# Inverse norms of queries and keys on GpSimd instead of ScalarE, and a new weaving of the instruction streams

## The chip, the cores and the metric

The kernel runs on one core of a Trainium2 chip. A core has five engines that run their own instruction lists in order: TensorE (PE, matrix multiplies and transposes), VectorE (DVE), ScalarE (ACT, one function per element), GpSimd (POOL) and SyncE (SP, which only issues DMA transfers here). They meet through semaphores. The metric is the device time of one execution in microseconds (us). Before the change it was 2464.19 us, the median of 3 runs (2455.86 to 2464.42).

## The reference, cut to what matters

The input is 16 elements (`b` below) of 512 tokens by 128 features. Each goes through a selective state space layer (the Mamba kind), then through two local attention layers with a feed-forward part each:

```python
x = x + layernorm(mamba(layernorm(x)))
h = layernorm(x)
for l in range(2):                          # "front" is l = 0, "back" is l = 1
    h = layer(h, ...)
x = x + layernorm(h)

# inside a layer
q, k, v = split(shift_token(h) @ wqkv)      # 8 heads of 64
q = q / clip(norm(q), 1e-12) * q_scale      # the part that the change moves
k = k / clip(norm(k), 1e-12) * k_scale
q, k = rotary_xpos(q, k)
o = local_attention(q * 8, k, v)            # windows of 64 tokens
h = h + o @ wo
h = h + feed_forward(shift_token(h))        # layernorm, gated GELU
```

The factor 8 on the queries is folded into the inverse norm. The state space layer is a scan over 512 steps for 256 channels with 16 states each.

## The kernel before, in words

The work on one element is cut into streams, each with a letter. `E` (enter) normalises the input, projects it and runs the short convolution; it ends with the step sizes. `F` (steps) makes the step sizes and their products with the input on POOL and sends them to memory. `M` (state) is the scan: 32 pieces of 128 partitions by 512 steps. For each piece POOL multiplies `dbu<-spread,bc` (the "feed"), ACT makes `da` by an exponential, DVE runs the scan `hs`, POOL multiplies `gy<-hs,bc` (the "read out"), and PE adds four of those into `y_sum`. `M` ends with two gates on POOL, a projection, two layer norms and `xs`, which is the input of `A` (front, layer 0). After it comes `B` (back, layer 1) and `C` (end: last norm, residual, store). `S` stores what `E` made for `M`.

While element `b` is in `B`, `b+1` is in `A`, `b+2` in `M` and `b+3` in `E`. Every engine works through one word per element. A word such as `A1 B2 M1` says: one step of stream A, two of B, one of M. So the order on each engine is written out by hand in the table `ORDER`, and an instruction that waits holds everything behind it on its engine. `AHEAD` says how many elements a stream is ahead, and `weave` plays the word; what is left of a stream at the end of a word is issued there. The streams in the code are functions named after engine and stream, for instance `act_attention` or `pool_state`.

A and B share no buffers. E shares PSUM bank and SBUF buffers with B: `x_pad` lies in B's `q_t`, `dt` and `du` in B's `k_t`, `dt_abs` in B's `m2`.

The inverse norms of a pair of token tiles (16 values per partition, 4 pairs in each of A and B) go through three engines. DVE sums squares (`ss`, line 879). POOL clips the sum from below (`clip`, line 952). ACT takes the logarithm (`lg`, line 810) and the exponential with scale -0.5 (`rn`, lines 815 and 817, the latter with a bias of log 8 for queries). POOL then multiplies the rotated tile by it (`normalise`, `kr<-kr,rn`, line 960). PE transposes the result, and ACT copies it to `q_t` or `k_t` (line 831). The sums of squares come from `square` on ACT (line 796) and the rotation from three DVE instructions per tile (lines 892, 896, 906). The projections are on line 703.

Of the kernel before, what the change touches and what calls it, by code (L numbers as in the profile page):

```python
# [15 lines left out]
P = 128  # L16
# [25 lines left out]
AHEAD = {"C": -1, "B": 0, "A": 1, "M": 2, "F": 2, "E": 3, "S": 3}  # L42
ORDER = {
# [4 lines left out]
    "act": (  # L48
# [4 lines left out]
    "dve": (  # L53
# [4 lines left out]
    "pool": (  # L58
        "F4 C1 A2 B1 A1 M2 B1 M2 B2 M3 B1 M1 A1 M1 B1 M1 B1 M1 A1 B1 M2 A1 M2 A1 B1 M1 B1 A1 B2 M3 A1 M3 A1 M1 A2 "
        "M44"),  # L60
    "sp": (
        "M1 F2 M5 A1 M1 B1 M1 E1 B1 M3 A1 M6 C1 M5 S3 B1"),
# [30 lines left out]
def weave(word, **streams):  # L93

    for part in word.split():
        for _ in range(int(part[1:]) if part[0] in streams else 0):
            next(streams[part[0]], None)
    for s in streams.values():
        for _ in s:
            pass  # L100


def build(nc, a, out):
    with ExitStack() as ctx:
# [35 lines left out]
        eps, log8 = (columns[:, n:n + 1] for n in range(2))  # L140
# [14 lines left out]
        class Attention:  # L155


            def __init__(self, n, banks, pr):
# [8 lines left out]
                self.lg = sb(f"lg{n}", [P, 8, HEADS])  # L167
# [416 lines left out]
        def act_state(E, e, b):  # L584
            if b > 0:
                E.wait_ge(*y_normed(b - 1))
            else:
                E.wait_ge(*a_made(0))
# [15 lines left out]
        def dve_state(E, e, b):  # L604
# [7 lines left out]

            for s in range(NSCAN):
# [164 lines left out]
        def act_attention(E, e, b, w, l):  # L778
# [10 lines left out]
            def square(take):  # L789
                n = ROPE.index(take)  # L790
                if entry and n == 0:
                    E.wait_ge(*e_turned(b + 2))
                E.wait_ge(*w.projected(b, projections.index(take)))
                if n > 1:
                    E.wait_ge(*w.summed(b, n // 2 - 1))
                e.activation(w.sq[:, n % 2, :], bank_of(take)[:, :], ACT.Square).then_inc(w.squared.sem, 1)  # L796
# [7 lines left out]

            def inverse_norms(g):

                part = lambda x: x[:, 2 * g:2 * g + 2, :]
                E.wait_ge(*w.clipped(b, g))
                E.use_table(EXP_LN)
# [3 lines left out]
                E.use_table(EXP_LN)  # L813
                if g % 2:
                    op = e.activation(part(w.rn), part(w.lg), ACT.Exp, scale=-0.5)
                else:
# [17 lines left out]
            for take in "q0 q1 v0 n0 k0 v1 k1 Q0 n1 Q1 q2 q3 v2 K0 n2 k2 K1 v3 k3 Q2 n3 Q3 K2 K3".split():  # L834
# [6 lines left out]
                elif take[0] == "n":  # L841
                    yield from inverse_norms(int(take[1]))
# [105 lines left out]
        def pool_attention(E, e, b, w):  # L948
            def clip(g):

                E.wait_ge(*w.summed(b, g))
                e.tensor_scalar(w.ss[:, 2 * g:2 * g + 2, :], w.ss[:, 2 * g:2 * g + 2, :], TINY, None, ALU.max).then_inc(
                    w.clipped.sem, 1)
# [9 lines left out]
            for take in "c0 q0 q1 c1 k0 k1 c2 q2 q3 c3 k2 k3".split():  # L963
                if take[0] == "c":
                    clip(int(take[1]))
# [169 lines left out]
        def dve_constants(E, e):  # L1135
            for column, value in ((eps, EPS), (log8, math.log(8.0))):
# [24 lines left out]
        def program(name, streams, once=None, at=0):  # L1161


            def body(e):
                E = Engine(e)
                for k in range(-3, B + 1):
                    if k == at and once:
                        once(E, e)
                    weave(ORDER[name], **{letter: stream(E, e, k + AHEAD[letter])
                                          for letter, stream in streams.items() if 0 <= k + AHEAD[letter] < B})  # L1170
# [9 lines left out]
        with nc.Block() as block:  # L1180
            block.sync(program("sp", dict(C=sp_end, B=sp_back, A=sp_front, M=sp_state, F=sp_steps, E=sp_enter, S=sp_spill)))
# [102 lines left out]
```

## Time and profile before

| what | value |
|---|---|
| median of 3 runs | 2464.19 us |
| the profiled execution's own time | 2461.61 us |
| its span, first to last instruction | 2459.8 us |
| PE busy | 1893.9 us (77%) |
| DVE busy | 1892.7 us (77%) |
| ACT busy | 1778.1 us (72%) |
| POOL busy | 1711.4 us (70%) |
| mean granted TensorE clock | 0.943 of full speed |

The busy shares are averages over the whole span. No engine is near 100%, so the page alone does not name a bound; within one element the engines take turns at being nearly full. Steady state repeats about every 140 us: the same pieces stand at 999.85 and at 1139.59 us. The chain of waits, followed back from the end, is 38% PE, 23% DVE, 13% ACT and 8% POOL.

### The profile page before, as it was taken

Reading aid. Unit: us, or ns where it says so; the run is one execution under the profiler, and the core shown is the slowest. Engines: PE = TensorE matmul, PEld = TensorE weight load, DVE = VectorE, ACT = ScalarE, POOL = GpSimd, SP = SyncE. Lnnn points to the kernel's source line nnn. Section 1 sums busy time; section 2 is a strip of 40 time slices with the busy share of each in tenths; the row PEclk is TensorE's granted clock in tenths of the full one; section 3 lists DMA queues with packets and bytes.
Section 4 is the critical chain, followed back from the end, with each engine's and each line's share of the span. In section 5 each row is a group of like instructions: output and inputs, shape, how many; then the busy total and the mean of one; then the engine's idle time right before and its main releaser. Section 6 shows DMA issues by size and latency. Waiting matters only on the chain.

```text
span 2459.8 us, 44075 instructions
## 1 busy us (share of the span) xinstructions
PE 1893.9 (77%) x15808; PEld 1114.3 (45%) x15936; DVE 1892.7 (77%) x3477; ACT 1778.1 (72%) x3955; POOL 1711.4 (70%) x1540
## 2 busy tenths in 40 slices
PE   2156778797878879797878879697888879787865
PEld 0013345353635445363635445363645545363634
DVE  3557797978879797988878797988879797887442
ACT  2245778696978878696878878696877869685644
POOL 1969595977959596886959596885959597792010
PEclk9977999899999989999999999999999989999988
DMA  4444443535344343534544353534543353531000
GB/s 162 126 120 115 112 105 104 132 83 146 103 130 117 100 121 92 134 86 131 129 129 103 103 124 96 138 87 130 130 115 99 110 127 90 137 99 33 17 20 9
DMA packets 126346, 261.09 MB, mean 106 GB/s; under 512 B 26928, under 2 KB 59696, under 8 KB 125872
## 3 DMA queue, kind: packets, MB, share of 16 engines
q1 hardware_dynamic: 126128, 258.27, 39.6%
q8 instruction: 126, 2.06, 0.4%
q14 instruction: 92, 0.75, 0.1%
HBM read 185.42 MB, written 42.99 MB: 93 GB/s over the span
## 4 chain that ended last, share of the span: by engine, by line
PE 38%; DVE 23%; ACT 13%; issue 9%; POOL 8%; DMA 4%; SPq 0%; DVEq 0%; POOLq 0%; ACTq 0%
DVE hs L618 6%; DVE m L892 4%; PE f_bank L342 4%; PE b_bank L342 4%; DVE kr L906 3%; POOL gy L663 3%; DMA spread<-steps 3%; POOL dbu L646 3%; ACT da L594 3%; PE b_bank L703 3%; PE f_bank L746 3%; PE y_sum L571 2%; DVE b_bank L896 2%; PE b_bank L773 2%; DVE ss L879 2%
## 5 line engine op out<-in xcount | busy, mean ns | idle before, releaser
L618 DVE TENSOR_TENSOR_SCAN hs<-da,dbu 128x512 f32<-128x512 f32 x512 | 622.2, 1215 | 127.1 <-POOL dbu L646 82.0
L663 POOL TENSOR_TENSOR gy<-hs,bc 128x512 f32<-128x512 f32 x512 | 652.1, 1274 | 41.5 <-DVE hs L618 31.2
L646 POOL TENSOR_TENSOR dbu<-spread,bc 128x512 f32<-128x512 f32 x512 | 651.5, 1274 | 9.1 <-DMA spread<-steps 9.0
L594 ACT ACTIVATE da<-spread,rest 128x512 f32<-128x512 f32 x512 | 359.4, 702 | 159.0 <-DVE hs L618 135.1
L703 PE MATMUL b_bank<-rest,h_t 128*128 128x512 f32 x384 | 227.9, 694 | 96.6 <-DVE kr L906 92.5
L960 POOL TENSOR_TENSOR kr<-kr,rn 128x512 f32<-128x512 f32 x256 | 264.8, 1043 | 42.3 <-ACT rn L817 37.0
L703 PE MATMUL f_bank<-rest,h_t 128*128 128x512 f32 x384 | 217.6, 665 | 72.1 <-DVE kr L906 64.2
L571 PE MATMUL y_sum<-gy,rest 128*32 128x512 f32 x1024 | 147.0, 649 | 92.4 <-POOL gy L663 92.3
L342 PE MATMUL f_bank<-first,kr 128*128 128x128 f32 x768 | 128.4, 298 | 78.9 <-DVE kr L906 49.8
L342 PE MATMUL b_bank<-first,kr 128*128 128x128 f32 x768 | 123.7, 296 | 57.8 <-DVE kr L906 41.8
L1106 POOL TENSOR_TENSOR xs<-xs,v 128x512 f32<-128x512 f32 x16 | 18.9, 1183 | 213.3 <-ACT xs L337 213.3
L417 POOL TENSOR_TENSOR k_t<-k_t,m 128x512 f32<-128x512 f32 x32 | 40.0, 1270 | 178.6 <-ACT m L494 178.6
L342 PEld LDWEIGHTS f_bank<-first,kr 128*128 128x128 f32 x768 | 93.3, 151 | 146.4 <-DVE kr L906 70.4
L857 ACT ACTIVATE late<-b_bank,mx 128x128 f32<-128x128 f32 x512 | 140.6, 383 | 23.8 <-DVE mx L922 23.8
L879 DVE TENSOR_REDUCE ss<-sq 128x16 f32<-128x1024 f32 x128 | 154.1, 1204 | 0.0
L342 PEld LDWEIGHTS b_bank<-first,kr 128*128 128x128 f32 x768 | 90.6, 150 | 140.0 <-DVE kr L906 67.3
L703 PEld LDWEIGHTS b_bank<-rest,h_t 128*128 128x128 f32 x384 | 70.7, 214 | 171.5 <-DVE kr L906 127.8
L857 ACT ACTIVATE sq<-f_bank,mx 128x128 f32<-128x128 f32 x512 | 144.0, 393 | 4.4 <-DVE mx L922 4.4
L703 PEld LDWEIGHTS f_bank<-rest,h_t 128*128 128x128 f32 x384 | 73.2, 212 | 158.4 <-DVE kr L906 92.4
L90 ACT ACT_TABLE_LOAD x82 | 105.2, 1283 | 20.4 <-DVE mv_enter L315 7.3
L892 DVE TENSOR_TENSOR m<-f_bank,tab 128x512 f32<-128x512 f32 x128 | 87.2, 682 | 39.1 <-ACT sq L796 39.0
L892 DVE TENSOR_TENSOR m<-b_bank,tab 128x512 f32<-128x512 f32 x128 | 87.2, 681 | 30.6 <-ACT sq L796 30.6
(168 smaller groups left out, 4748.2 us busy)
## 6 DMA issues: line engine op xcount, KB each, us to landing
spread<-steps SPq DMA_DIRECT2D x256, 512.0 KB, 5.1
vs<-v SPq DMA_DIRECT2D x96, 260.0 KB, 5.9
bc<-bc_rows SPq DMA_DIRECT2D x32, 512.0 KB, 6.2
steps<-k_t SPq DMA_DIRECT2D x32, 512.0 KB, 2.7
gate<-gates SPq DMA_DIRECT2D x32, 512.0 KB, 5.7
gates<-kr SPq DMA_DIRECT2D x16, 512.0 KB, 3.4
gates<-late SPq DMA_DIRECT2D x16, 512.0 KB, 4.3
vs<-v SPq DMA_DIRECT2D x32, 130.0 KB, 4.5
```

Of the source, the lines that this page charges most:

```text
L90: self.e.preload_act_table_set(name)
L342: op = e.transpose(bank[:, n * P:(n + 1) * P], src(n), ident[:, :])
L571: op = e.matmul(y_sum[32 * j:32 * j + 32, :], sel[:, w, :], gy[:, 2 * j + k, :], start=w == 0 and k == 0, stop=w == 1 and k == 1, skip_gro ...
L594: e.activation(da[:, :], spread[:, slot(b, s // 2), 0, :], ACT.Exp, scale=a_neg[:, s:s + 1]).then_inc(decayed.sem, 1)
L618: e.tensor_tensor_scan(hs[:, s % 2, :], da[:, :], dbu[:, s % 2, :], 0.0, ALU.mult, ALU.add).then_inc(scanned.sem, 1)
L646: e.tensor_tensor(dbu[:, s % 2, :], spread[:, slot(b, s // 2), 1, :], bc[:, s % 2, :], ALU.mult).then_inc(fed.sem, 1)
L663: e.tensor_tensor(gy[:, s % 8, :], hs[:, s % 2, :], bc[:, 2 + s % 2, :], ALU.mult).then_inc(read_out.sem, 1)
L703: e.matmul(bank[:, :], w.h_t[:, t * P:(t + 1) * P], wqkv[:, l, part * INNER:(part + 1) * INNER], start=True, stop=True).then_inc(w.project ...
L857: op = e.activation(w.pr[:, hd % 2, p, :], X[hd % 2][:, p * P:(p + 1) * P], ACT.Exp, bias=w.mx[:, hd, p:p + 1])
L879: e.tensor_reduce(w.ss[:, 2 * g:2 * g + 2, :], w.sq[:, :, :].rearrange("p n (h d) -> p n h d", h=HEADS), AX, ALU.add).then_inc(w.summed.se ...
L892: e.tensor_tensor(halves(w.m2[:, n % 2, :]), halves(bank[:, :])[:, :, ::-1, :], table[1], ALU.mult).then_inc(w.rotated.sem, 1)
L960: e.tensor_tensor(x, x, w.rn[:, n, :].unsqueeze(2).to_broadcast([P, HEADS, DH]), ALU.mult).then_inc(w.normed.sem, 1)
```

## The change

It does three things.

1. The logarithm and exponential of the inverse norms leave ACT (`inverse_norms` is gone, and 8 steps of each ACT attention stream with it). POOL now follows its clip with a `tensor_tensor` of the operation power: `ss` to the power of a column that holds -1/2. To keep the factor 8 of the queries, ACT squares them with a scale of 0.125. Buffer `lg` is gone.
2. `weave` no longer starts and ends each stream within a word. A stream is now one chain over all 16 elements, the word is repeated until all chains are out, and a second string says how many turns a stream lets pass at the start. `AHEAD` is gone. The set-up work of ACT and DVE (`act_tables`, `dve_tables`) moves to the first step of `M`.
3. All five words are new. They begin at another point of the element's cycle, and most of their text is the old order rotated to it.

```diff
 class Engine / weave
-def weave(word, **streams):
-    for part in word.split():
-        for _ in range(int(part[1:]) if part[0] in streams else 0):
-            next(streams[part[0]], None)
-    for s in streams.values():
-        for _ in s:
-            pass
+def weave(word, late, **chains):
+    late = {part[0]: int(part[1:]) for part in late.split()}
+    while chains:
+        for part in word.split():
+            for _ in range(int(part[1:])):
+                if late[part[0]]:
+                    late[part[0]] -= 1
+                elif part[0] in chains and next(chains[part[0]], chains) is chains:
+                    del chains[part[0]]
...
-        eps, log8 = (columns[:, n:n + 1] for n in range(2))
+        eps, root = (columns[:, n:n + 1] for n in range(2))
...
-                e.activation(w.sq[:, n % 2, :], bank_of(take)[:, :], ACT.Square).then_inc(w.squared.sem, 1)
+                e.activation(w.sq[:, n % 2, :], bank_of(take)[:, :], ACT.Square, scale=0.125 if take[0] == "q" else 1.0).then_inc(
+                    w.squared.sem, 1)
...
-            def inverse_norms(g):
-                part = lambda x: x[:, 2 * g:2 * g + 2, :]
-                E.wait_ge(*w.clipped(b, g))
-                e.activation(part(w.lg), part(w.ss), ACT.Ln).then_inc(w.logged.sem, 1)
-                yield
-                E.wait_ge(*w.logged(b, g))
...
-                    op = e.activation(part(w.rn), part(w.lg), ACT.Exp, scale=-0.5, bias=log8)
-                op.then_inc(w.inverse.sem, 1)
-                yield
...
-            for take in "q0 q1 v0 n0 k0 v1 k1 Q0 n1 Q1 q2 q3 v2 K0 n2 k2 K1 v3 k3 Q2 n3 Q3 K2 K3".split():
+            for take in "q0 q1 v0 k0 v1 k1 Q0 Q1 q2 q3 v2 K0 k2 K1 v3 k3 Q2 Q3 K2 K3".split():
...
         def pool_attention(E, e, b, w):
-            def clip(g):
+            def inverse_roots(g):
+                part = lambda x: x[:, 2 * g:2 * g + 2, :]
                 E.wait_ge(*w.summed(b, g))
-                e.tensor_scalar(w.ss[:, 2 * g:2 * g + 2, :], w.ss[:, 2 * g:2 * g + 2, :], TINY, None, ALU.max).then_inc(
-                    w.clipped.sem, 1)
+                e.tensor_scalar(part(w.ss), part(w.ss), TINY if g % 2 else TINY / 64, None, ALU.max).then_inc(w.clipped.sem, 1)
+                E.wait_ge(*w.clipped(b, g))
+                e.tensor_tensor(part(w.rn), part(w.ss), root.unsqueeze(2).to_broadcast([P, 2, HEADS]), ALU.pow).then_inc(
+                    w.inverse.sem, 1)
...
         "sp" word
-        "M1 F2 M5 A1 M1 B1 M1 E1 B1 M3 A1 M6 C1 M5 S3 B1"),
+        "M1 B1 M3 E1 M1 B1 M2 A1 M1 A1 M9 S3 M1 B1 F1 M1 F1 M2 C1 M1",
+        "A4 B9 C3 E0 F0 M18 S0"),
```

How the order moved is seen best in the instruction lists. On POOL, at the start of a new pair of attentions (steady state), this stood in a row before: `xs<-xs,v` ends stream C, `ss<-ss` is a clip, `kr<-kr,rn` a normalisation.

```order
L1106 TENSOR_TENSOR xs<-xs,v 128x512
L952 TENSOR_SCALAR ss<-ss 128x16
L960 TENSOR_TENSOR kr<-kr,rn 128x512
L952 TENSOR_SCALAR ss<-ss 128x16
L960 TENSOR_TENSOR kr<-kr,rn 128x512
L646 TENSOR_TENSOR dbu<-spread,bc 128x512 x2
L960 TENSOR_TENSOR kr<-kr,rn 128x512
L663 TENSOR_TENSOR gy<-hs,bc 128x512
```

And this stands there now; `rn<-ss,columns` is the power.

```order
L1098 TENSOR_TENSOR xs<-xs,v 128x512
L942 TENSOR_SCALAR ss<-ss 128x16
L944 TENSOR_TENSOR rn<-ss,columns 128x16
L952 TENSOR_TENSOR kr<-kr,rn 128x512 x2
L653 TENSOR_TENSOR dbu<-spread,bc 128x512
L942 TENSOR_SCALAR ss<-ss 128x16
L944 TENSOR_TENSOR rn<-ss,columns 128x16
L653 TENSOR_TENSOR dbu<-spread,bc 128x512
L952 TENSOR_TENSOR kr<-kr,rn 128x512
L670 TENSOR_TENSOR gy<-hs,bc 128x512
```

Eight powers per element are new on POOL, each directly behind its clip; both normalisations of A's first pair now come before the first feed.

On ACT, from the norm of `x1` (end of stream M) to the first squares of the next pair of attentions, this stood before. `m<-m` are the four functions of stream F, `h_t` is the shifted input of an attention (`f_bank` is A, `b_bank` is B), `lv_out` and `rs_out` belong to C.

```order
L326 ACTIVATE rs_x<-lv_x 128x4
L337 ACTIVATE xs<-x,mr_x,rs_x 128x128 x4
L484 ACTIVATE m<-b_bank,first 128x512
L491 ACTIVATE m<-m 128x512 x2
L494 ACTIVATE m<-m 128x512 x2
L783 ACTIVATE h_t<-f_bank 64x512
L785 ACTIVATE h_t<-f_bank 64x511
L783 ACTIVATE h_t<-b_bank 64x512
L785 ACTIVATE h_t<-b_bank 64x511
L796 ACTIVATE sq<-f_bank 128x512
L322 ACTIVATE lv_out<-mv_out,columns 128x4
L326 ACTIVATE rs_out<-lv_out 128x4
```

This stands there now.

```order
L330 ACTIVATE rs_x<-lv_x 128x4
L488 ACTIVATE m<-b_bank,first 128x512
L495 ACTIVATE m<-m 128x512 x2
L498 ACTIVATE m<-m 128x512 x2
L341 ACTIVATE xs<-x,mr_x,rs_x 128x128 x4
L326 ACTIVATE lv_out<-mv_out,columns 128x4
L330 ACTIVATE rs_out<-lv_out 128x4
L790 ACTIVATE h_t<-f_bank 64x512
L792 ACTIVATE h_t<-f_bank 64x511
L790 ACTIVATE h_t<-b_bank 64x512
L792 ACTIVATE h_t<-b_bank 64x511
L803 ACTIVATE sq<-f_bank 128x512
```

The norm of `x1` moved behind F, and C's two small instructions moved ahead of the attention inputs. DVE has the matching move: `stat_out` and `mv_out` now stand before the last addition of A's feed-forward, not behind it.

On SP the load of the read-out factors (`bc<-bc_rows`, the second of its kind) stood right behind the first two groups of step sizes:

```order
L376 DMA steps<-k_t 128x2x512
L379 DMA steps<-k_t 128x2x512
L514 DMA spread<-steps 128x1x1024 x2
L508 DMA bc<-bc_rows 128x1x1024
L514 DMA spread<-steps 128x1x1024 x2
```

Now the store of the finished element, which waits for `xs<-xs,v` on POOL, stands between them:

```order
L383 DMA steps<-k_t 128x2x512
L518 DMA spread<-steps 128x1x1024 x2
L1115 DMA out_dram<-xs 128x4x128
L512 DMA bc<-bc_rows 128x1x1024
L518 DMA spread<-steps 128x1x1024
```

The second load of factors and all behind it now wait for the end of C.

## Rows read from the trace of the kernel before

**Rows 1.** Busy time by stage of one element (front, heads, tail), in us.

```profile
1121.00:1182.00 61.00, 43.07 (x239) 21.22 (x240) 56.34 (x89) 40.49 (x93) 50.61 (x52) 0.92 0.56 139
1182.00:1235.00 53.00, 48.19 (x641) 34.48 (x645) 46.44 (x91) 48.30 (x120) 50.82 (x42) 1.00 0.38 101
1235.00:1261.00 26.00, 24.60 (x117) 13.29 (x114) 14.53 (x40) 21.89 (x38) 6.07 (x5) 1.00 0.28 83
```

**Rows 2.** The residual addition that ends M: durations, first and last start.

```profile
L674 POOL TENSOR_TENSOR x<-gy,x x16: 1261/1270/1274, 152.0 to 2221.8; 128x512 f32<-128x512 f32 x16
```

**Rows 3.** The chain of waits from 1129 to 1181 us: start, length, what.

```profile
1129.20 0.59 DVE m L892
...
1156.17 0.60 ACT k_t L831
1156.77 0.11 ACT lg L810
...
1156.91 0.32 ACT rn L817
...
1157.29 1.04 POOL kr L960
...
1179.99 1.01 POOL kr L960
```

**Rows 4.** Groups by line and shape: count, busy us, mean ns, idle before.

```profile
L663 POOL TENSOR_TENSOR gy<-hs,bc 128x512 f32<-128x512 f32 x512 | 652.1, 1274 | 41.5 <-DVE hs L618 31.2 <-DMA bc<-bc_rows 5.0 <-PE y_sum L571 1.0
L960 POOL TENSOR_TENSOR kr<-kr,rn 128x512 f32<-128x512 f32 x256 | 264.8, 1043 | 42.3 <-ACT rn L817 37.0 <-ACT rn L815 3.1 <-DVE kr L906 0.6
L952 POOL TENSOR_SCALAR ss<-ss 128x16 f32<-128x16 f32 x128 | 31.4, 245 | 93.2 <-DVE ss L879 92.6
L810 ACT ACTIVATE lg<-ss 128x16 f32<-128x16 f32 x128 | 27.3, 213 | 49.2 <-POOL ss L952 48.5
L817 ACT ACTIVATE rn<-lg,columns 128x16 f32<-128x16 f32 x64 | 19.7, 307 | 2.1
L815 ACT ACTIVATE rn<-lg 128x16 f32<-128x16 f32 x64 | 13.8, 216 | 2.0
```

**Rows 5.** POOL in order of time, front stage: start, length, idle before.

```profile
1131.00 0.24 POOL L952 TENSOR_SCALAR ss<-ss 128x16 f32<-128x16 f32 x1 [1.09 <-DVE ss L879]
1131.92 1.04 POOL L960 TENSOR_TENSOR kr<-kr,rn 128x512 f32<-128x512 f32 x1 [0.67 <-ACT rn L817]
...
1142.67 0.24 POOL L952 TENSOR_SCALAR ss<-ss 128x16 f32<-128x16 f32 x1 [1.39 <-DVE ss L879]
...
1153.04 0.24 POOL L952 TENSOR_SCALAR ss<-ss 128x16 f32<-128x16 f32 x1 [0.54 <-DVE ss L879]
...
1157.29 1.04 POOL L960 TENSOR_TENSOR kr<-kr,rn 128x512 f32<-128x512 f32 x1 [1.77 <-ACT rn L817]
...
1178.52 0.24 POOL L952 TENSOR_SCALAR ss<-ss 128x16 f32<-128x16 f32 x1 [0.16 <-DVE ss L879]
```

**Rows 6.** Who waited for whom from 1121 to 1182 us: total, times, longest.

```profile
DVE m L892 <- ACT sq L796: 3.5, 3, 1.7
```

**Rows 7.** End of M and start of the next attentions, in order of time.

```profile
1115.35 1.65 ACT L337 ACTIVATE xs<-x,mr_x,rs_x 128x128 f32<-128x128 f32 x4 [0.64 <-DVE mr_x L331]
...
1117.48 1.14 ACT L491 ACTIVATE m<-m 128x512 f32<-128x512 f32 x2
...
1120.48 0.60 PE L342 MATMUL f_bank<-first,xs 128*128 128x128 f32 x4
```

**Rows 8.** The second load of factors, C's last step, and the first read out.

```profile
1128.22 0.60 SPq L508 DMA_DIRECT2D bc<-bc_rows  x1
...
1128.73 1.18 POOL L1106 TENSOR_TENSOR xs<-xs,v 128x512 f32<-128x512 f32 x1 [4.58 <-ACT xs L337]
...
1137.78 1.27 POOL L663 TENSOR_TENSOR gy<-hs,bc 128x512 f32<-128x512 f32 x1
```

**Rows 9.** DMA issues on the page: count, KB each, us from issue to landing.

```profile
bc<-bc_rows SPq DMA_DIRECT2D x32, 512.0 KB, 6.2
```

More of the change, by code:

```diff
@@ L35 @@
 ROPE = "q0 q1 k0 k1 q2 q3 k2 k3".split()
-AHEAD = {"C": -1, "B": 0, "A": 1, "M": 2, "F": 2, "E": 3, "S": 3}
 ORDER = {
     "pe": (
[3 rows of a table removed]
[4 rows of a table added]
     "act": (
[4 rows of a table removed]
-    "dve": (
[4 rows of a table removed]
[5 rows of a table added]
+    "dve": (
[5 rows of a table added]
     "pool": (
-        "F4 C1 A2 B1 A1 M2 B1 M2 B2 M3 B1 M1 A1 M1 B1 M1 B1 M1 A1 B1 M2 A1 M2 A1 B1 M1 B1 A1 B2 M3 A1 M3 A1 M1 A2 "
-        "M44"),
+        "M2 F4 C1 A3 M1 B1 M1 B1 M2 B1 M1 B2 M3 A1 M2 A1 M2 B2 M1 A1 M1 B2 M1 A1 M1 A1 B3 M2 A1 M5 A3 M42",
+        "A12 B24 C3 F0 M2"),
     "sp": (
-        "M1 F2 M5 A1 M1 B1 M1 E1 B1 M3 A1 M6 C1 M5 S3 B1"),
+        "M1 B1 M3 E1 M1 B1 M2 A1 M1 A1 M9 S3 M1 B1 F1 M1 F1 M2 C1 M1",
+        "A4 B9 C3 E0 F0 M18 S0"),
 }
@@ L166, in __init__ @@
                 self.ss = sb(f"ss{n}", [P, 8, HEADS])
-                self.lg = sb(f"lg{n}", [P, 8, HEADS])
                 self.rn = sb(f"rn{n}", [P, 8, HEADS])
@@ L587, in act_state @@
             else:
+                act_tables(E, e)
                 E.wait_ge(*a_made(0))
@@ L611, in skip @@
                                        ALU.add).then_inc(skipped.sem, 1)
+            if b == 0:
+                dve_tables(E, e)
             for s in range(NSCAN):
@@ L803, in value @@
                 e.activation(w.v[:, t, :, 0:DH], heads(bank_of(take)[:, :]), ACT.Copy).then_inc(w.v_copied.sem, 1)
-            def inverse_norms(g):
-                part = lambda x: x[:, 2 * g:2 * g + 2, :]
-                E.wait_ge(*w.clipped(b, g))
-                E.use_table(EXP_LN)
-                e.activation(part(w.lg), part(w.ss), ACT.Ln).then_inc(w.logged.sem, 1)
-                yield
-                E.wait_ge(*w.logged(b, g))
[L813 to L816, printed above, removed]
-                    op = e.activation(part(w.rn), part(w.lg), ACT.Exp, scale=-0.5, bias=log8)
-                op.then_inc(w.inverse.sem, 1)
-                yield
             def channel_major(take):
@@ L840, in act_attention @@
                     yield
-                elif take[0] == "n":
-                    yield from inverse_norms(int(take[1]))
                 else:
@@ L964, in pool_attention @@
                 if take[0] == "c":
-                    clip(int(take[1]))
+                    inverse_roots(int(take[1]))
                 else:
@@ L1135, in dve_constants @@
         def dve_constants(E, e):
-            for column, value in ((eps, EPS), (log8, math.log(8.0))):
+            for column, value in ((eps, EPS), (root, -0.5)):
                 e.memset(column, value)
@@ L1159, in act_tables, with program, elements @@
             e.activation(a_neg[:, :], a_neg[:, :], ACT.Exp).then_inc(a_exp.sem, 1)
-        def program(name, streams, once=None, at=0):
+        def program(name, **streams):
+            def elements(E, e, stream):
+                for b in range(B):
+                    yield from stream(E, e, b)
             def body(e):
                 E = Engine(e)
[L1166 to L1170, printed above, removed]
+                weave(*ORDER[name], **{letter: elements(E, e, stream) for letter, stream in streams.items()})
                 if name == "sp":
@@ L1180, in build @@
         with nc.Block() as block:
-            block.sync(program("sp", dict(C=sp_end, B=sp_back, A=sp_front, M=sp_state, F=sp_steps, E=sp_enter, S=sp_spill)))
-            block.gpsimd(program("pool", dict(C=pool_end, B=pool_back, A=pool_front, M=pool_state, F=pool_steps)))
-            block.scalar(program("act", dict(C=act_end, B=act_back, A=act_front, M=act_state, F=act_steps, E=act_enter),
-                                 act_tables, -2))
-            block.vector(program("dve", dict(C=dve_end, B=dve_back, A=dve_front, M=dve_state, E=dve_enter), dve_tables, -2))
-            block.tensor(program("pe", dict(B=pe_back, A=pe_front, M=pe_state, E=pe_enter)))
+            block.sync(program("sp", C=sp_end, B=sp_back, A=sp_front, M=sp_state, F=sp_steps, E=sp_enter, S=sp_spill))
+            block.gpsimd(program("pool", C=pool_end, B=pool_back, A=pool_front, M=pool_state, F=pool_steps))
+            block.scalar(program("act", C=act_end, B=act_back, A=act_front, M=act_state, F=act_steps, E=act_enter))
+            block.vector(program("dve", C=dve_end, B=dve_back, A=dve_front, M=dve_state, E=dve_enter))
+            block.tensor(program("pe", B=pe_back, A=pe_front, M=pe_state, E=pe_enter))
 FIRST = [("ident", (P,)), ("w_in", (2 * DI,)), ("conv_w", (NH2, NCONV)), ("conv_b", (NH2,)), ("w_x", (NH2, 2 * NS + RANK)),
```

25 rows, old and new, of the table ORDER are left out of this document.

## The prediction

> **What bounds the kernel now.** I read the busy times by stage first, then the chain of waits, then POOL in order of time.
>
> One element takes about 140 us and falls into three stages [rows 1]; the columns are PE, weight loads, DVE, ACT, POOL. In the front stage (projections, rotation, norms) DVE is busy 56.3 of 61 us and POOL 50.6. In the stage of the heads POOL is busy 50.8 of 53, ACT 48.3 and PE 48.2. In the tail PE is busy 24.6 of 26 and POOL 6.1. So the edit falls in the front stage, where DVE is fullest, and it loads POOL, the fullest engine of the next one.
>
> POOL's idle time in the front stage is at its beginning: it cannot start before the first clip at 1131.00, and from there it runs almost without a break to 1181.0, 50.0 us [rows 3, 5]. The chain of waits goes through the other engines up to 1156, then ACT's copy of a key tile, logarithm and exponential, and from 1157.29 to 1181.0 it is POOL alone, 23.7 us [rows 3]. Five gaps interrupt the 50.0 us: 0.67 + 1.39 + 0.54 + 1.77 + 0.16 = 4.53 us [rows 5]. Two of them (0.67 and 1.77) end with ACT's exponential. The 1.77 is the telling one: the clip of that pair was over at 1153.28, but ACT's logarithm stood behind a copy that ran only at 1156.17, so the inverse norm was there at 1157.2 [rows 3, 5].
>
> **Taken from ACT.** Per full element 8 logarithms and 8 exponentials: over the run 27.3 + 19.7 + 13.8 = 60.8 us of busy time [rows 4], 3.8 us per element, and 48.5 / 16 = 3.0 us in which ACT stood for the clip [rows 4]. Little of this is on the path: where the chain crosses them it is 0.11 + 0.32 us [rows 3]. It frees ACT's queue, so squares come earlier, and DVE's wait for squares (3.5 us per front stage [rows 6]) can shrink. I count nothing for it beside POOL's gain below, since both end the same stage; the cap on any gain in the front stage is DVE's idle time there, 61 - 56.3 = 4.7 us [rows 1].
>
> **Added to POOL.** 8 powers of 128x16 per element. No row shows a power. From below: a clip of the same shape takes 245 ns [rows 4]. From above I take a whole 128x512 multiplication, 1274 ns [rows 4]. The nearest row is the clip, same engine and shape; a power is more work on each of the 16 elements. The multiplication by the inverse norm costs 1043 ns for 512 elements [rows 4], 2.0 ns each; with five times that for a power, 16 x 10 = 160 ns, I take 0.40 us as an estimate. Eight make 3.2 us, all of it inside POOL's 50 us run.
>
> The Trainium skill, "GPSIMD Engine Reference", Performance versus the Vector engine, puts a two-input elementwise body at about 2.6 cycles per element and data-dependent branching at about 12, and says to keep elementwise work off this engine. At its 1.2 GHz the first is 2.2 ns; the row gives 2.0, so they agree. By 12 cycles a power of 16 elements would be 0.16 us over the fixed part; by the plain body the whole would be about 0.28 us, and the eight 2.2 us.
>
> **The stall that goes.** With the power behind its clip on POOL, the two gaps that end with ACT cannot occur. The other three end with DVE's sum of squares; as POOL gets busier in between, they close too. Sum over the run: -4.53 + 3.2 = -1.3 us per element. What is late next: DVE, full in this stage, and POOL itself. If the powers cost more than 4.53 / 8 = 0.57 us, POOL's run gets longer than before.
>
> **What the new words do.** On DVE the sum of squares of A's first pair has one instruction fewer ahead of it, a step of 0.6 us (a 128x512 instruction of the rotation holds the chain for 0.59 [rows 3]). POOL's run begins that much earlier: -0.6 us. C's small instructions go ahead of the attention inputs on ACT, and C's statistics ahead of A's last addition on DVE, so POOL's `xs` comes earlier, and ACT waits less for it before it copies B's values. That wait is off the chain; I count it at zero.
>
> The norm of `x1` moves behind F on ACT. It began at 1115.35; one function of about 0.6 us and F, two pairs of 1.1 us each, now stand ahead, so it would end near 1119.8, and PE reads it at 1120.48 [rows 7]. The work of PE that lies before that transpose hides it with 0.7 us to spare; before there were 3.5. F, no longer behind 1.65 us of norm [rows 7], starts some 1.5 us earlier, and so do the stores of the step sizes.
>
> SP's second load of factors was issued at 1128.22. It now waits for C's last POOL step, over at 1129.91, so about 2 us later. Such a load takes 6.2 us [rows 9]: it lands near 1136.5, and the first read out was at 1137.78 [rows 8]. Hidden by 1.3 us; if `xs` is late, M's start pays it one for one. Behind this load stand two groups of step sizes, of which the first pieces are already there.
>
> **Start and end.** M ends 16 times, from 152.0 to 2221.8 us [rows 2]. Full front stages with A, B and M together number 14. After 2222 there is one A with a B, then a B alone; there POOL is not full, and a pair costs the hop from clip to normalisation. That was 0.92 us (1131.00 to 1131.92 [rows 5]); now it is 0.24 + 0.40 plus a small gap, about 0.7. Twelve hops save 2 us. The repeated word changes neither which stream runs beside which nor how many instructions there are, so I count the new weaving itself at zero, with 5 us either way.
>
> **The sum.** (-1.3 - 0.6) x 14 = -27, and -2 at the end: 2461.6 - 29 = 2433 us. The profiled execution's own 2461.6 is 0.1% below the median of the runs shown, 2464.2, so the figure holds for both.
>
> **Rivals.**
>
> *The power is expensive (slower).* One mechanism: a power of 1.0 us, between the bounds. Place: POOL's run in the front stage. Price: 8.0 - 4.53 - 0.6 = +2.9 us per element, x 14 = +40, so 2502 us; at 1.27 us it would be +5.1 x 14 = +71, so 2533. It decides from 0.57 us (0.65 with the earlier start). For it: the chain is POOL alone for the last 23.7 us, three clips lie in that part, and POOL has only 2.2 us of room in the stage of the heads. Against it: M's end has 3.5 us of room before PE, so POOL may drag scan work into the tail before the cycle lengthens; this may swallow part.
>
> *No change.* The powers take just what the gaps give, or DVE's 56.3 us in the front and PE's 24.6 in the tail hold the cycle wherever POOL stands: 2461 us, within 0.5% of now. For it: neither engine loses an instruction. Against it: the chain does not go through DVE after 1157.
>
> *The words bring more.* ACT and DVE, no longer held by POOL's clips, give most of the 4.7 us cap: -3.3 us per element, x 14 = -46, so 2415 us. For it: ACT loses 6.8 us of work and waiting in this stage. Against it: the 3.5 us that DVE waited for squares partly end with PE's projections, which the edit does not touch.
>
> *The change doesn't do what it says.* Excluded: the instruction lists show 8 powers and no logarithm or exponential for them, and as many loads of function tables as before.
>
> **How the numbers follow.** Chances: my forecast 0.38, the words bring more 0.12, no change 0.17, expensive power 0.33. A difference of 0.5% (12 us) is about what a measurement can tell from none. So faster 0.50, same 0.17, slower 0.33. The range must reach into the expensive power: up to 2506, a power of 1.0 us with a few us; what lies above is the dearer part of that case. Below it reaches to 2402, the third rival with words and start 13 us better. The forecast's own range is 2415 to 2448.
>
> **What would show it.** The power's mean on its own row decides most: 0.40 right, over 0.65 wrong. POOL from its first clip of a front stage to its last normalisation: 50.0 us before, about 48.7 after. The wait of the normalisation for ACT (40.1 us) must be gone, and so ACT's 48.5 us for the clip. ACT's busy time falls by 61 us; POOL's rises by 128 x 0.40 = 51. DVE's wait for POOL's feeds must not rise; if it does, POOL became the bound. PE's transpose of `xs` must still not wait for the norm of `x1`, nor the first read out for the second load of factors. M's ends must span less than the 2069.8 us that lie between the first and the last now. I am wrong if that distance grows.

## The result, and the profile of the changed kernel

The changed kernel takes 2773.14 us (median of 4 runs, 2771.90 to 2775.28), against 2464.31 us before (median of 4, 2455.86 to 2468.20): 1.126 times as long, 95% interval 1.1243 to 1.1276. The profiled execution's span is 2770.1 us, +310 on before's 2459.8. I had forecast 2433 us and a range up to 2506. The place that I gave in the first rival was right, POOL's run in the front stage; the price of a power was not, and that price alone carries the result.

The groups by line, on the page of the changed kernel (busy us, mean ns of one, idle before and what ended it), which answer to [rows 4]:

```profile
L625 DVE TENSOR_TENSOR_SCAN hs<-da,dbu 128x512 f32<-128x512 f32 x512 | 623.6, 1218 | 299.7 <-POOL dbu L653 245.7
L944 POOL TENSOR_TENSOR rn<-ss,columns 128x16 f32<-128x16 f32 x128 | 374.2, 2924 | 10.7
L346 PE MATMUL b_bank<-first,kr 128*128 128x128 f32 x768 | 149.5, 341 | 292.2 <-POOL kr L952 272.4
L952 POOL TENSOR_TENSOR kr<-kr,rn 128x512 f32<-128x512 f32 x256 | 263.9, 1042 | 5.4
```

A power of 128x16 takes 2.924 us, more than two 128x512 multiplications (1.27 us). The 128 of them are 374.2 us of POOL. The normalisation waits for nobody now: 5.4 us of idle time before it, 42.3 before [rows 4]. Instead DVE's scan waits 245.7 us for POOL's feeds and PE's transposes of stream B wait 272.4 us for POOL's normalised tiles. Before, these two waits were 82.0 and 10.0 us:

```profile
L618 DVE TENSOR_TENSOR_SCAN hs<-da,dbu 128x512 f32<-128x512 f32 x512 | 622.2, 1215 | 127.1 <-POOL dbu L646 82.0 <-ACT da L594 36.8 <-POOL gy L663 3.6
L342 PE MATMUL b_bank<-first,kr 128*128 128x128 f32 x768 | 123.7, 296 | 57.8 <-DVE kr L906 41.8 <-POOL kr L960 10.0 <-ACT v L803 4.9
```

The chain that ended last, by engine and by line: before, POOL had 8% of it, now 43%, and the power alone has 13%. The 43% is not all the power's doing: in the run below with a multiplication in its place POOL has 34% of the chain, and that kernel is not slower than before. What the power adds is its own 13%.

```profile
POOL 43%; PE 27%; DVE 11%; ACT 6%; issue 6%; DMA 0%; POOLq 0%; SPq 0%; DVEq 0%; ACTq 0%
POOL rn L944 13%; POOL gy L670 12%; POOL dbu L653 11%; POOL kr L952 6%; DVE hs L625 4%; PE f_bank L346 3%; PE b_bank L346 3%; PE y_sum L575 2%; DVE m L882 2%; PE f_bank L986 2%; PE b_bank L992 2%; PE f_bank L983 2%; PE f_bank L992 1%; PE b_bank L736 1%; ACT late L847 1%
```

The stages of one element, cut at the same events as in [rows 1] (columns PE, weight loads, DVE, ACT, POOL, then the granted clock of PE): the front took 61 us and takes 81, the other two 54 and 26 as against 53 and 26. In the front POOL is busy 72.2 us where it was 50.6; DVE, which I had named as the fullest there, has 58.0 us of work in it (56.3 before) and 20 us more for it.

```profile
1256.00:1337.00 81.00, 46.36 (x238) 23.61 (x239) 57.97 (x82) 37.68 (x78) 72.20 (x58) 0.85 0.42 109
1337.00:1391.00 54.00, 49.08 (x638) 36.54 (x644) 44.34 (x90) 47.29 (x116) 51.55 (x42) 0.97 0.39 102
1391.00:1417.00 26.00, 25.08 (x121) 13.38 (x120) 16.02 (x47) 22.61 (x40) 7.22 (x6) 1.00 0.20 63
```

POOL in order of time in that front stage (start, length), which answers to [rows 5]: eight powers, each just behind its clip, the last before the two normalisations with which the stage ends.

```profile
1266.13 0.25 POOL L942 TENSOR_SCALAR ss<-ss 128x16 f32<-128x16 f32 x1 [1.35 <-DVE ss L869]
1266.46 2.92 POOL L944 TENSOR_TENSOR rn<-ss,columns 128x16 f32<-128x16 f32 x1
1269.47 2.04 POOL L952 TENSOR_TENSOR kr<-kr,rn 128x512 f32<-128x512 f32 x2
1271.47 1.26 POOL L653 TENSOR_TENSOR dbu<-spread,bc 128x512 f32<-128x512 f32 x1
1272.81 0.25 POOL L942 TENSOR_SCALAR ss<-ss 128x16 f32<-128x16 f32 x1
1273.15 2.92 POOL L944 TENSOR_TENSOR rn<-ss,columns 128x16 f32<-128x16 f32 x1
...
1332.81 2.92 POOL L944 TENSOR_TENSOR rn<-ss,columns 128x16 f32<-128x16 f32 x1
1335.81 2.04 POOL L952 TENSOR_TENSOR kr<-kr,rn 128x512 f32<-128x512 f32 x2
```

From the first clip at 1266.13 to the end of the first of the last two normalisations (1336.86) it is 70.7 us; before, the same stretch was 50.0. The account closes: 8 powers of 2.92 and 8 small gaps of 0.08 before them are 24.0, less the five gaps of [rows 5], 4.53, plus one new idle time of 0.76 us, make +20.3 of the measured +20.7. The ends of M, against [rows 2]:

```profile
L681 POOL TENSOR_TENSOR x<-gy,x x16: 1262/1272/1277, 150.5 to 2525.5; 128x512 f32<-128x512 f32 x16
```

First to last it is 2375.0 us, 2069.8 before: +305.2 over 15 elements, 20.3 each. That this distance grows was my sign of being wrong. With +6.6 behind the last M and -1.5 before the first, that is the whole +310.

### The profile page after: what moved, and what is told of

Same layout as the page of the kernel before. It is cut to its first block, busy times and chain, and to the rows that moved or that the text cites. A ratio compares the mean times of both kernels' runs of the same rounds, so it can differ in the third digit from the quotient of the medians.

```text
span 2770.1 us, 43947 instructions
## 1 busy us (share of the span) xinstructions
PE 1967.0 (71%) x15808; PEld 1176.3 (42%) x15936; DVE 1911.2 (69%) x3477; ACT 1728.2 (62%) x3699; POOL 2085.5 (75%) x1668
## 4 chain that ended last, share of the span: by engine, by line
POOL 43%; PE 27%; DVE 11%; ACT 6%; issue 6%; DMA 0%; POOLq 0%; SPq 0%; DVEq 0%; ACTq 0%
POOL rn L944 13%; POOL gy L670 12%; POOL dbu L653 11%; POOL kr L952 6%; DVE hs L625 4%; PE f_bank L346 3%; PE b_bank L346 3%; PE y_sum L575 2%; DVE m L882 2%; PE f_bank L986 2%; PE b_bank L992 2%; PE f_bank L983 2%; PE f_bank L992 1%; PE b_bank L736 1%; ACT late L847 1%
## 5 line engine op out<-in xcount | busy, mean ns | idle before, releaser
L625 DVE TENSOR_TENSOR_SCAN hs<-da,dbu 128x512 f32<-128x512 f32 x512 | 623.6, 1218 | 299.7 <-POOL dbu L653 245.7
L944 POOL TENSOR_TENSOR rn<-ss,columns 128x16 f32<-128x16 f32 x128 | 374.2, 2924 | 10.7
L346 PE MATMUL b_bank<-first,kr 128*128 128x128 f32 x768 | 149.5, 341 | 292.2 <-POOL kr L952 272.4
L346 PE MATMUL f_bank<-first,kr 128*128 128x128 f32 x768 | 156.8, 345 | 173.5 <-DVE kr L896 107.6
L346 PEld LDWEIGHTS b_bank<-first,kr 128*128 128x128 f32 x768 | 105.9, 172 | 389.1 <-issue 329.4
L346 PEld LDWEIGHTS f_bank<-first,kr 128*128 128x128 f32 x768 | 117.0, 179 | 220.9 <-DVE kr L896 125.9
L1098 POOL TENSOR_TENSOR xs<-xs,v 128x512 f32<-128x512 f32 x16 | 18.9, 1181 | 223.2 <-ACT xs L341 223.2
L823 ACT ACTIVATE k_t<-b_bank 128x512 f32<-128x512 f32 x64 | 38.2, 597 | 165.0 <-PE b_bank L346 165.0
```

The lines of the kernel that those rows point to most:

```text
L346: op = e.transpose(bank[:, n * P:(n + 1) * P], src(n), ident[:, :])
L625: e.tensor_tensor_scan(hs[:, s % 2, :], da[:, :], dbu[:, s % 2, :], 0.0, ALU.mult, ALU.add).then_inc(scanned.sem, 1)
L944: e.tensor_tensor(part(w.rn), part(w.ss), root.unsqueeze(2).to_broadcast([P, 2, HEADS]), ALU.pow).then_inc(w.inverse.sem, 1)
```

## The experiments

Three questions: is it the power (its price, or its place), the new words, or the new weaving? The ratios are against the kernel before, with 95% intervals.

### A multiplication in the power's place

```diff
-  e.tensor_tensor(part(w.rn), part(w.ss), root..., ALU.pow)
+  e.tensor_tensor(part(w.rn), part(w.ss), root..., ALU.mult)
```

> The changed kernel with a multiplication in the place of the power (the norms are left out, all instructions and waits stay). Price theory: the instruction takes about 0.25 us, and the time is that of my prediction's formula, 8 x 0.34 - 4.53 - 0.6 = -2.4 us per element x 14: 2420 to 2450 us. Place rival (two dependent GpSimd instructions and the hop to them cost, whatever they compute): above 2550 us.

This kernel leaves the inverse norms out: a multiplication stands where they were made. 2445.82 us, ratio 0.9938 (0.9915 to 0.9960). All else is the changed kernel: same words, waits and number of instructions. The row of that instruction and the scan's wait for feeds:

```profile
L944 POOL TENSOR_TENSOR rn<-ss,columns 128x16 f32<-128x16 f32 x128 | 27.8, 217 | 10.7
L625 DVE TENSOR_TENSOR_SCAN hs<-da,dbu 128x512 f32<-128x512 f32 x512 | 623.0, 1217 | 123.5 <-POOL dbu L653 79.4 <-ACT da L599 37.5 <-issue 5.3
```

The operation alone is worth 2773.1 - 2445.8 = 327.3 us, 2.56 us for each of 128, of the 2.71 by which the two instructions differ. The instruction in its place, with the words and the weaving, is harmless, even 0.6% faster than before.

This run also shows what the new words do to POOL's run in the front stage. From the first clip (1122.97) to the end of the first of the last two normalisations it takes 49.3 us, 50.0 before. All five gaps of [rows 5] are gone; one new idle time stands before the first read out, with no releaser that the profile shows. The ends of M lie 2052.1 us apart, 1.2 us less per element than before:

```profile
1130.67 1.27 POOL L670 TENSOR_TENSOR gy<-hs,bc 128x512 f32<-128x512 f32 x1 [0.94 <-issue]
L681 POOL TENSOR_TENSOR x<-gy,x x16: 1263/1272/1277, 150.6 to 2202.7; 128x512 f32<-128x512 f32 x16
```

### The power with the old words

The kernel before, with the logarithm and exponential gone from ACT (empty steps stand for them, so the words stay as they are) and the power behind the clip on POOL; the factor 8 moves to the squares, as in the change.

```diff
-  e.activation(part(w.lg), part(w.ss), ACT.Ln) ... e.activation(part(w.rn), part(w.lg), ACT.Exp, scale=-0.5)
+  yield; yield                                  # ACT: two empty steps
+  e.tensor_tensor(part(w.rn), part(w.ss), root..., ALU.pow)   # POOL, behind the clip
```

> The kernel before with its own weaving and words; only the edit of the norms is made: power on GpSimd behind the clip, two empty ScalarE steps where logarithm and exponential stood. Price theory: 8 x (2.92 + 0.09) - 4.5 = 19.6 us more per element, x 15 to 16, so 2755 to 2780 us. Order rival: the power alone explains less, so below 2700 us.

2821.24 us, ratio 1.1460 (1.1439 to 1.1480). So the power is at least as dear with the old words, and the new ones take 48 us off it. The time lies 41 us above the range of the price theory (2755 to 2780), so the sum with the measured power was too low here. Per element it is 3.1 us more than in the changed kernel. The trace shows 2.3 of them: the first clip comes 0.6 us later behind the end of M, and POOL's run lasts 72.4 us against 70.7, with two gaps left that DVE's sum of squares ends (0.88 and 1.33 us). The rest is open. The wait that shows it is DVE's for feeds, 336.5 us here against 245.7 in the changed kernel:

```profile
L618 DVE TENSOR_TENSOR_SCAN hs<-da,dbu 128x512 f32<-128x512 f32 x512 | 622.9, 1217 | 403.2 <-POOL dbu L646 336.5
```

### The multiplication with the old words

The same with `ALU.mult` for `ALU.pow`; again the inverse norms are left out.

> The kernel before with its own weaving and words and a multiplication where the power would be (the norms are left out), ScalarE without logarithm and exponential. With e2 it gives the price of the power under the old words; with e3 what the new words are worth when the instruction is cheap. If the hop over ScalarE was what the old words paid for: below before, 2420 to 2450 us. If the old words fit only with the hop: 2455 to 2500 us. In both cases e2 minus e11 should be that of the changed kernel minus e3, about 327 us.

2459.67 us, ratio 0.9987 (0.9978 to 0.9997). With the run above it tests my term "the stall that goes". POOL's rows, and three clips of one front stage:

```profile
L954 POOL TENSOR_TENSOR kr<-kr,rn 128x512 f32<-128x512 f32 x256 | 264.0, 1043 | 2.3
L944 POOL TENSOR_SCALAR ss<-ss 128x16 f32<-128x16 f32 x128 | 31.3, 244 | 96.1 <-DVE ss L870 91.6
L946 POOL TENSOR_TENSOR rn<-ss,columns 128x16 f32<-128x16 f32 x128 | 27.7, 216 | 10.7
...
1140.90 0.24 POOL L944 TENSOR_SCALAR ss<-ss 128x16 f32<-128x16 f32 x1 [1.38 <-DVE ss L870]
...
1152.11 0.24 POOL L944 TENSOR_SCALAR ss<-ss 128x16 f32<-128x16 f32 x1 [0.80 <-DVE ss L870]
...
1176.72 0.24 POOL L944 TENSOR_SCALAR ss<-ss 128x16 f32<-128x16 f32 x1 [0.16 <-DVE ss L870]
```

The idle time before the normalisation falls from 42.3 [rows 4] to 2.3 us, but 27.7 + 10.7 us of new instruction and gap take almost all of it, and the idle time before the clips, which DVE ends, does not close: 96.1 against 93.2. In the front stage the two gaps that ACT ended are gone, the three that DVE ended stand (2.34 us, 2.09 before), and POOL's run is 50.3 us, 50.0 before. I had let all five gaps go; with the old words only two do.

### The new words with ACT's functions

The changed kernel, with logarithm and exponential on ACT again, issued just ahead of the next step of the attention stream, and no power.

```diff
+  E.wait_ge(*w.clipped(b, g)); e.activation(part(w.lg), part(w.ss), ACT.Ln)
+  E.wait_ge(*w.logged(b, g));  e.activation(part(w.rn), part(w.lg), ACT.Exp, scale=-0.5)
-  e.tensor_tensor(part(w.rn), part(w.ss), root..., ALU.pow)
```

> The changed kernel with its weaving and its words, but the logarithm and the exponential back on ScalarE (issued ahead of the step that follows) and no power on GpSimd. Price theory (the 2.92 us of a power on GpSimd's full queue is the whole loss): back to the level of before, 2430 to 2470 us. Order rival (the new words cost a good part of the 309 us): above 2520 us.

2557.57 us, ratio 1.0388 (1.0369 to 1.0407). My price theory failed, and the time lies in the range of the rival (above 2520): I had thought the words independent of where the inverse norm is made. POOL now stands for ACT (42.3 us before [rows 4]):

```profile
L961 POOL TENSOR_TENSOR kr<-kr,rn 128x512 f32<-128x512 f32 x256 | 264.5, 1045 | 120.9 <-ACT rn L820 120.8
```

In the new word of POOL four of the eight clips of a front stage have their own normalisation right behind them. With POOL's own instruction between them POOL waits for nobody, with a hop to ACT and back it stands and holds the scan's feeds meanwhile: DVE waits 113.3 us for them, 79.4 with the multiplication. In one front stage these waits for ACT are 7.6 us, in five places; before they were the 2.4 us of two gaps [rows 5]. The four corners and their partners, in us:

| | logarithm and exponential on ACT | multiplication on POOL | power on POOL |
|---|---|---|---|
| old words | 2461 (before, in the run beside) | 2460 | 2821 |
| new words | 2558 | 2446 | 2773 |

Power less multiplication is 361.6 us in one row and 327.3 in the other. The power is dear with either words; that the two differences should be the same, as I had expected, is off by 34 us.

### The new words with ACT's functions and no clip

The logarithm adds a small constant instead (`bias=tiny`) and waits for DVE's sum alone.

> The new words and the new weaving, logarithm and exponential on ACT ahead of the next step of the stream, and no clip: the logarithm adds a small constant instead, so that it waits for DVE's sum of squares alone and POOL has nothing in that chain before the normalisation. It asks what makes the new words dear with ACT's functions (2557.6 us against 2461). Theory 1, the hop: POOL's clip, placed in the new words just ahead of the normalisations, starts the chain late, and POOL then stands for ACT. Without the clip most of the 96 us are back: 2465 to 2490 us, and POOL's wait of kr for ACT's rn, 120.8 us there, falls below 40. Theory 2, ACT's queue: the functions have no steps of their own in ACT's new word and stand behind copies and exponentials, so that rn is late whoever clips. Then it stays at 2540 to 2560 us and the wait for rn stays over 90 us.

2502.27 us, ratio 1.0167 (1.0152 to 1.0182). It lies between the two theories: 55 of the 96 us come back, so the hop over POOL's clip is a little more than half of it, and some 40 stay. The sign of the first theory was plainly wrong, and that of the second right: POOL's wait for `rn` rose, from 120.8 to 170.0 us. POOL's idle time before clips and normalisations together hardly changed (74.3 + 120.9 us there, 196.8 here), so this wait alone does not say what a kernel loses.

```profile
L961 POOL TENSOR_TENSOR kr<-kr,rn 128x512 f32<-128x512 f32 x256 | 263.9, 1043 | 196.8 <-ACT rn L820 170.0 <-DVE kr L908 26.8
```

The same edit on the kernel before, tried as a version that might beat both:

> A version meant to beat both: the kernel before, where ScalarE's logarithm takes the lower bound as its bias (log of the sum plus 1e-24) and GpSimd's 128 clips are gone. The chain is then VectorE, ScalarE, GpSimd without the first GpSimd turn. If GpSimd's run in the front stage and the hop count: 8 x 0.2 = 1.6 us less per element and less waiting of ScalarE, 2420 to 2450 us. If VectorE and TensorE hold the cycle wherever GpSimd stands: within 0.5% of before.

2461.39 us, ratio 0.9999 (0.9989 to 1.0010). Without its 128 clips POOL only waits longer for the inverse norms, 106.9 + 13.1 us against 37.0 + 3.1 [rows 4]:

```profile
L960 POOL TENSOR_TENSOR kr<-kr,rn 128x512 f32<-128x512 f32 x256 | 264.5, 1042 | 142.5 <-ACT rn L817 106.9 <-DVE kr L906 22.3 <-ACT rn L815 13.1
```

### The new weaving alone

The kernel before with the new `weave`, its second string of turns, and the moved set-up. The instruction lists are those of before but for two rows of ACT's set-up.

```diff
-def weave(word, **streams):   # streams of one element, rest issued at the word's end
+def weave(word, late, **chains):   # one chain over 16 elements, the word repeated
```

> The kernel before with the new weaving alone: each stream one chain over all 16 elements, the words repeated, a second string of turns let pass at the start, the function tables and constants made in the first step of M. The words are the old ones and the instruction lists are those of before but for two rows of set-up on ACT. Theory 1, as I forecast: the weaving costs nothing, 2456 to 2466 us. Rival: the weaving or the moved set-up shifts the streams against each other at the start, over 5 us either way.

2462.70 us against 2462.64, ratio 1.0002 (0.9992 to 1.0011): the weaving costs nothing, as forecast.

### Two powers for one

```diff
+  e.tensor_tensor(part(w.lg), part(w.ss), root..., ALU.pow)
   e.tensor_tensor(part(w.rn), part(w.ss), root..., ALU.pow)
```

> The changed kernel with one more power per pair, of the same operands into a scratch tile. Price theory: GpSimd's queue is already the bound in the front stage, so each of the 128 extra powers costs its whole 2.92 us: 2773 + 374 = about 3147 us (3110 to 3160). Place rival (what costs is that a power stands between clip and normalisation, not its length): below 2950 us.

3145.34 us, ratio 1.2773 (1.2745 to 1.2801): +372.2 us over the changed kernel for 128 further powers of 2.895 us (370.6 us). At this load POOL's time goes into the total one for one.

```profile
L946 POOL TENSOR_TENSOR rn<-ss,columns x128: 2892/2895/2900, 174.9 to 3070.3; 128x16 f32<-128x16 f32 x128
```

### The power in two halves, and in other sizes

Two powers of 128x8 in place of one of 128x16:

```diff
-  e.tensor_tensor(part(w.rn), part(w.ss), root..., ALU.pow)
+  for i in range(2):
+      e.tensor_tensor(w.rn[:, 2 * g + i, :], w.ss[:, 2 * g + i, :], root..., ALU.pow)
```

> The changed kernel with each power of 128x16 cut into two of 128x8. If the 2.92 us are a cost per element (0.17 us each over 0.2 us): two of about 1.56 us, and the whole is 2785 to 2815 us. If they are mostly a fixed cost of calling the power: two of 2.9 us, and the whole is near 3100 us.

2824.54 us, ratio 1.1471 (1.1448 to 1.1494), which is +51.4 over the changed kernel; by the rows it is 128 x (2 x 1.648 - 2.924) = +47.6.

```profile
L945 POOL TENSOR_TENSOR rn<-ss,columns 128x8 f32<-128x8 f32 x256 | 418.0, 1648 | 10.7
```

A third kernel is the changed one with five probes on POOL ahead of its first wait:

```diff
+  e.tensor_tensor(1 element, ALU.mult);  e.tensor_tensor(1 element, ALU.pow)
+  e.tensor_tensor(16, ALU.mult);  e.tensor_tensor(16, ALU.pow);  e.tensor_tensor(64, ALU.pow)
```

> The changed kernel with six small GpSimd instructions ahead of everything, while GpSimd is idle for its first 40 us: multiplications of 128x1 and 128x16, powers of 128x1, 128x16 (exponent from a full tile, base 2.0) and 128x64. Cost per element: 0.4, 2.9 and about 11 us. Fixed cost: about 2.8, 2.9 and 3.2 us. The whole time stays within 0.5% of 2773 us either way.

One run, 2772.44 us. POOL in order of time (start, length):

```profile
2.17 0.19 POOL L1166 TENSOR_TENSOR gy<-gy 128x1 f32<-128x1 f32 x1
2.44 0.56 POOL L1168 TENSOR_TENSOR gy<-gy,columns 128x1 f32<-128x1 f32 x1
3.07 0.22 POOL L1170 TENSOR_TENSOR gy<-gy 128x16 f32<-128x16 f32 x1
3.37 2.91 POOL L1172 TENSOR_TENSOR gy<-gy 128x16 f32<-128x16 f32 x1
6.36 10.52 POOL L1174 TENSOR_TENSOR gy<-gy,columns 128x64 f32<-128x64 f32 x1
```

From 1 to 64 elements per partition the power rises by (10.52 - 0.56) / 63 = 0.158 us each, and 0.40 us is left as the fixed part. Size 8 fits (0.40 + 1.26 = 1.66, measured 1.648) and size 16 (2.93). A base and an exponent of 2.0, both from a tensor (fourth row), cost what real sums of squares with -1/2 from a broadcast column do: 2.91 us, and all 128 powers of the changed kernel lie between 2.923 and 2.929 us.

### The power in A only

Stream A with the power on POOL, stream B with ACT's functions, new words.

```diff
+  if w is wf:    # stream A
       e.tensor_tensor(part(w.rn), part(w.ss), root..., ALU.pow)
```

> The changed kernel with powers in stream A only (4 per element); stream B has logarithm and exponential on ScalarE again. Price theory, linear: half of the way between e1 and the changed kernel, 2600 to 2620 us. If GpSimd has slack that swallows the first powers: 2500 to 2570 us. If only stream B's chain of dependent steps matters: near e1.

2667.41 us, ratio 1.0837 (1.0817 to 1.0857), above the 2600 to 2620 that I expected. It lies in the middle between the kernels with no power (2557.6) and with all (2773.1): +110 and +106. My low figure took the new words to be good with ACT's functions, which the run with ACT's functions denies.

### A power where POOL is idle

The kernel before, its queries and keys untouched; only the inverse standard deviations of the two norms that end M are a power of 128x4 on POOL, in the tail.

```diff
-  yield from act_norm_scale(E, e, n_y, b)      # ACT: logarithm and exponential; the same for n_x
+  e.tensor_scalar(w.lv, w.mv[:, :, 1], EPS, None, ALU.add)    # POOL
+  e.tensor_tensor(w.rs, w.lv, root..., ALU.pow)
```

> The kernel before, with the inverse norms of its queries and keys untouched, and a power of 128x4 for the inverse standard deviations of the two layer norms that end stream M, in place of ACT's logarithm and exponential; POOL does them in the tail, where it is busy 6.1 of 26 us. Theory 1, a power costs about 0.40 us plus 0.158 us for each element of a row, so here 1.03 us, twice per element, and it pays only where POOL has nothing else and the next engine waits for less than it did: an activation pair of 128x4 costs about 0.4 to 0.7 us with its hops on ACT, so the chain in the tail gets 0.4 to 0.8 us longer per norm while ACT's queue is relieved: 2455 to 2480 us, within 0.5% of before or just above. Theory 2, place is all and cost nothing: ACT is the crowded one there, and the tail gets 1 to 2 us shorter per element: 2430 to 2445 us. Theory 3, any power on POOL costs as in the changed kernel, its duration times 32 or more: 2494 us or more.

2474.65 us, ratio 1.0051 (1.0037 to 1.0065). The length came as worked out from the sizes, 1.03 us:

```profile
L676 POOL TENSOR_TENSOR rs_x<-lv_x,columns 128x4 f32<-128x4 f32 x16 | 16.6, 1037 | 1.3
L676 POOL TENSOR_TENSOR rs_y<-lv_y,columns 128x4 f32<-128x4 f32 x16 | 16.6, 1036 | 1.3
```

The whole edit costs 12 us, although ACT has 37 us less to do (1740.9 us busy against 1778.1). I read it as the power being on the path of those that wait for it; no run with a multiplication there separates the power from the hop to POOL, so the split is not shown. No version of mine beats the kernel before by a measurable amount with the norms it has to compute.

## Why the prediction was wrong, step by step

**The price of a power: the step that failed.** The step is "Added to POOL". "With five times that for a power, 16 x 10 = 160 ns, I take 0.40 us as an estimate. Eight make 3.2 us." Measured: 2.924 us, eight make 23.4. An element costs 158 ns, not 10: 78 times the 2.0 ns of the multiplication in [rows 4], where I had allowed for five times. My upper bound was wrong in kind. I took the time of a 128x512 multiplication as a ceiling, but it bounds the price of sixteen powers only if one power costs less than 32 multiplications, and no row said so. Nothing in the trace bounded it from above; the honest range was open, and then the range of the time too.

By the Trainium skill's figure for data-dependent branching, about 12 cycles per element ("GPSIMD Engine Reference", Performance versus the Vector engine), the estimate was 0.16 us for the power over its fixed part; measured it is 2.52 us, 16 times that, and the measurement decides.

**The formula that I put beside it was nearly good.** With the measured price, the sum of the prediction gives 8 x (2.92 + 0.08) - 4.53 - 0.6 = +18.9 us per element; measured +20.3. The sum took 14 elements, which would give +264, or about 2724 us, 49 below the measured time; all 15 distances between the ends of M grew, so 15 is the right count (+283, measured +305). The rival "the power is expensive" named place and sign, and its own price of 1.0 us was too low by a factor of three. Its escape ("POOL may drag scan work into the tail") is not taken: the tail holds 7.2 us of POOL's work, 6.1 before [rows 1]. The doubled power shows that at this load every microsecond of POOL counts once.

**"The stall that goes" held only with the new words.** I took off 4.53 us per element and gave as the reason that POOL gets busier in between. In the changed kernel all five gaps are gone, and the account above closes with the full 4.53. With a multiplication for the power it depends on the words. The new words lose all five as well. The old words lose only the two that ended with ACT; the three that ended with DVE's sum of squares stand, at 2.34 us. So at a cheap price it was not POOL's load that closed them but the order, and the term belonged to the new words. What it lacked is on the other side: an inserted multiplication takes 0.22 us and a gap of 0.08, and the new words bring an idle time of 0.94 us before the first read out. So with a price of 0.22 us my sum gives (-4.53 + 8 x 0.22 - 0.6) = -3.4 us per element, and the run with the multiplication shows -1.2. This error of about 2 us per element is hidden in the result behind the other.

**The break-even was too generous.** I gave 0.57 us. Between the two measured points of the new words (2445.8 us at 0.217, 2773.1 at 2.924) a microsecond of the instruction costs 121 us of the run; a straight line meets 2461 us at 0.34 us. That is an estimate. For a straight line speaks that the distance between the ends of M grows as much as the instructions do: by 21.5 us per element for 8 x 2.71 = 21.7, and by 22.9 for the 23.2 of the doubled power. By it, even at my own 0.40 us the change would have stood near 2468 and not at 2433.

**The new words.** With the multiplication they gain 12 (by the ratios) to 14 us over the old ones, about 0.9 per element. The 0.6 us that I gave them came to the hundredth: in steady state the first clip starts 22.27 us after the last addition of M in the kernel before and 21.68 in the changed one. The norm of `x1`, which I had end near the transposes of PE, did not delay them, and the second load of factors, now issued behind C's last step, was no wait for the first read out (1278.27 in the timeline, load issued 1265.23). With the multiplication the read out comes earlier; there the load, issued at 1122.08, took 7.1 us and landed at about 1129.2, before POOL was free at 1129.73, so the 0.94 us that POOL then stands are not shown to be the load's. In the changed kernel both covers held:

```profile
1253.52 1.64 ACT L341 ACTIVATE xs<-x,mr_x,rs_x 128x128 f32<-128x128 f32 x4
...
1256.21 0.60 PE L346 MATMUL f_bank<-first,xs 128*128 128x128 f32 x4
```

What I missed is that the words and the power belong together: with ACT's functions they cost 96 us. More than half of that is the hop over POOL's clip; what makes the other 41 us is open beyond the row that shows POOL waiting for ACT. I placed the functions ahead of other steps there, so part may be this placing.

**The weaving** at zero: right (1.0002). **ACT's busy time** fell by 49.9 us to 1728.2, not by 61; the rest is in ACT's other instructions. POOL's rose by 374, the 128 powers to the microsecond.

## What to carry to other kernels

An operation that no row of the trace shows has no upper bound from a cheaper operation's rows, however large these are: either measure one instruction of it first, or let the range stay open and give the slow side the larger chance. The test that would have settled this case is one instruction long (a power of 128x16, 2.91 us). And before an operation moves to another engine for its queue's sake, work out what one microsecond more on that engine costs: here 0.95 us (new words) to 1.04 us (old words) for each microsecond by which POOL's instruction grows, while taking some 50 us off ACT and putting 38 us on POOL, in the old words, gave 4 us or less.

## What the runs showed of the hardware

- A `tensor_tensor` power on POOL takes 0.40 us and 0.158 us per element of a partition's row: 0.56 us for 1, 1.04 for 4, 1.65 for 8, 2.92 for 16, 10.52 for 64. The multiplication takes 0.19 us for 1 and 0.22 for 16. The same inverse root as logarithm and exponential on ACT is 0.21 + 0.22 to 0.31 us for 16 [rows 4].
- The length did not change with the values that these runs used: 2.923 to 2.929 us over 128 powers with exponent -1/2, 2.91 us for base and exponent 2.0. Other values were not tried.
- PE was granted 0.85 of the full clock on average in the front stage, 0.92 before, so part of the stretch ran at the lower of its two levels (1.2 and 2.4 GHz), and it stands there for POOL's tiles; its transposes take 341 ns in place of 296 ns. Over the run PE is busy 73 us more with the same products (1967.0 against 1893.9; both traces lack records of 128 of the 15936 products). I read that as a consequence of the waiting and not as the cause: with the multiplication, in the same words and with all records there, PE is busy 1926.8 us.
